# FP4 quantisers of a two-layer audio tower: the rounding constant sized by ScalarE, in a new order of all engines

## The reference, cut to what matters

```python
_GRID = [0.0, 0.5, 1.0, 1.5, 2.0, 3.0, 4.0, 6.0]
_MID  = [0.25, 0.75, 1.25, 1.75, 2.5, 3.5, 5.0]

def fp4_quant_dequant(x):                       # blocks of 16 along the last dim
    scale = max(max(abs(xb)) / 6.0, 1e-12)
    xn = xb / scale
    q = _GRID[searchsorted(_MID, abs(xn))] * sign(xn) * scale

h = silu(fp4_linear(x, w_gate)) * fp4_linear(x, w_up)     # 256 -> 704
return fp4_linear(h, w_down)                              # 704 -> 256
```

## Time and profile before

| | |
|---|---|
| median of 3 runs | 325.51 us (325.51 to 326.44) |
| profiled execution | span 326.4 us, own time 326.44 us |
| TensorE busy | 303.4 us, 5142 matmuls |
| VectorE busy | 240.5 us, 519 instructions |
| ScalarE busy | 121.4 us, 267 instructions |
| GpSimd busy | 26.1 us |
| mean granted TensorE clock | 0.989 |

### The profile page before, as it was taken

One profiled execution on the slowest core, in us unless ns is written; L12 is line 12 of the kernel. 1 busy time (PEld: TensorE's weight loads), 2 busy tenths in 40 slices (PEclk: granted clock), 3 DMA queues, 4 the chain that ended last, 5 costly groups with the idle time before them and its releaser, 6 DMA issues.

```text
span 326.4 us, 11811 instructions
## 1 busy us (share of the span) xinstructions
PE 303.4 (93%) x5142; PEld 265.7 (81%) x5142; DVE 240.5 (74%) x519; ACT 121.4 (37%) x267; POOL 26.1 (8%) x50
## 2 busy tenths in 40 slices
...
GB/s 244 323 329 262 1 3 100 34 4 2 2 52 19 2 4 2 2 1 2 16 21 4 2 4 2 2 4 3 5 16 18 2 4 4 5 0 0 2 0 64
DMA packets 8821, 12.80 MB, mean 39 GB/s; under 512 B 826, under 2 KB 5698, under 8 KB 8772
## 3 DMA queue, kind: packets, MB, share of 16 engines
q1 hardware_dynamic: 8772, 12.06, 11.2%
...
...
## 4 chain that ended last, share of the span: by engine, by line
PE 81%; DVE 10%; DMA 3%; issue 3%; ACT 1%; SPq 1%; POOL 0%; DVEq 0%; ACTq 0%
PE psum L1226 71%; PE psum L1416 2%; DMA ffw_raw<-in_L_ffn_aux_weight_dram 2%; PE psum L1542 2%; PE psum L1438 1%; DMA tokw_raw<-in_L_tok_W_dram 1%; PE psum L1297 1%; PE psum L1322 1%; DVE qs L846 1%; DVE hha L849 1%; DVE qma L1174 1%; PE psum L1253 1%; PE psum L1345 1%; ACT qma L759 1%; PE psum L1519 1%
## 5 line engine op out<-in xcount | busy, mean ns | idle before, releaser
L555 POOL TENSOR_TENSOR ln_rs<-ln_mv,minus_half 128x1 f32<-128x1 f32 x40 | 24.9, 628 | 262.4 <-DVE ln_mv L917 262.4
L1226 PE MATMUL psum<-aT_hi,wqkv_hi 128*128 128x256 f32 x128 | 37.5, 293 | 0.4 <-DVE xT_lo L865 0.2
L1226 PE MATMUL psum<-aT_lo,wqkv_hi 128*128 128x256 f32 x128 | 36.1, 282 | 0.0
L1226 PE MATMUL psum<-aT_hi,wqkv_lo 128*128 128x256 f32 x128 | 35.9, 280 | 0.0
L570 ACT ACTIVATE qkT<-psum 128x512 f32<-128x512 f32 x32 | 18.9, 598 | 36.2 <-PE psum L1226 36.0
L1226 PE MATMUL psum<-wout_s,oT 128*128 128x256 f32 x128 | 29.4, 383 | 0.0
L1226 PEld LDWEIGHTS psum<-wout_s,oT 128*128 128x128 f32 x128 | 23.7, 190 | 3.4
L1226 PEld LDWEIGHTS psum<-aT_hi,wqkv_hi 128*128 128x128 f32 x128 | 24.1, 188 | 1.2 <-issue 0.9
L1226 PEld LDWEIGHTS psum<-aT_lo,wqkv_hi 128*128 128x128 f32 x128 | 24.1, 188 | 0.0
L1226 PEld LDWEIGHTS psum<-aT_hi,wqkv_lo 128*128 128x128 f32 x128 | 24.1, 188 | 0.0
L1226 PE MATMUL psum<-bias_parts,pick_r 128*128 128x256 f32 (+1 forms) x40 | 15.1, 378 | 6.2 <-DVE tokw_lo L865 1.6
...
## 6 DMA issues: line engine op xcount, KB each, us to landing
...
w_raw<-in_L_attn_W_qkv_dram SPq DMA_DIRECT2D x1, 768.0 KB, 10.2
...
```

Source lines behind the costliest of these rows:

```text
L555: nc.gpsimd.tensor_tensor(ln_rs[:, s, k, j:j + 1], ln_mv[:, s, k, j, 1:2], minus_half[:, :], ALU.pow).then_inc(rstd_ready[f"{k}_{j}"], 1)
L1226: return nc.tensor.matmul(o_, a, b, start=first, stop=last)
```

## The change

Steps d and e go. ScalarE computes m = |v| * (2^22 - 1) from the scaled v in one ACTIVATE with Abs, for all four kinds of array: `size_w` (w0e, w1e, w2e in ScalarE's list), `size` (ye and he). VectorE's f becomes max(m, MAGIC) + v and g becomes max(m, MAGIC) - v, the negative of the rounded value, so h multiplies by -1 and by the scale. f, g and h are scalar_tensor_tensor everywhere. VectorE's c signals ScalarE (`scaled`), and f waits for ScalarE (`sized`). A memset on GpSimd and the exponents' semaphores go. All five lists are new: the same steps otherwise, 304 of TensorE, 234 instead of 223 of ScalarE, 388 instead of 418 of VectorE, 41 of GpSimd and 11 of the DMA queue.

```diff
 MAGIC = 1.5 * 2.0 ** 22
+TO_MAGIC = 2.0 ** 22 - 1.0
 BELOW_ONE = float(np.float32(1 - 2.0 ** -24))
...
-        turn_tok xT0.0 bcast warm5 tok0.0 warm3 xT1.0 warm4 tok1.0 warm2 xT0.1 warm1 warm0 turn_ff tok0.1 aT.0
-        join_ff1 xT1.1 qk7.0 qk1.0 tok1.1 qk3.0 v00.0 v01.0 v12.0 qk4.0 qk0.0 qk5.0 v02.0 qk2.0 v11.0 qk6.0
...
+        warm5 warm3 turn_tok xT0.0 xT1.0 warm4 tok0.0 bcast tok1.0 warm2 warm1 xT0.1 warm0 aT.0 turn_ff tok0.1
+        xT1.1 join_ff1 qk1.0 qk7.0 tok1.1 qk3.0 v12.0 v01.0 qk4.0 v00.0 qk5.0 qk0.0 v02.0 qk2.0 v10.0 qk6.0
...
+        g0_1.3 hT0_0.2 g1_1.3 u0_1.3 hT1_0.2 u1_1.3 hT0_1.2 down_0.2 hT1_1.2 hT0_0.3 down_1.2 hT1_0.3 down_0.3
+        hT0_1.3 tail3 hT1_1.3 down_1.3 tail0 tail2""",
...
+        tables turn_tok xT0.0 xT1.0 split_qkv2 bcast split_qkv0 split_qkv3 split_qkv1 split_qkv4 split_b xT0.1
+        aT.0 split_qkv5 turn_ff xT1.1 qk1.0 qk7.0 qk3.0 v12.0 v01.0 qk4.0 v00.0 w0e qk5.0 qk0.0 v02.0 join_ff1
+        qk2.0 v10.0 qk6.0 v11.0 xT0.2 s0.0 e0.0 aT.1 turn_gate1 w1e join_ff2 v00.1 split_w1 s1.0 oT00.0 w2e
+        qk4.1 e1.0 qk3.1 qk6.1 qk2.1 turn_gate0 qk5.1 oT01.0 qk0.1 qk7.1 qk1.1 turn_up1 s0.1 turn_up0 e0.1
...
+        ye_0.2 o1T_0.3 exp1_1.3 o1T_1.2 val1_1.3 yT_0.2 ye_0.3 g0_0.2 g1_0.2 yT_0.3 ye_1.2 o1T_1.3 g0_0.3 yT_1.2
+        g1_0.3 g0_1.2 g1_1.2 ye_1.3 he_0.2 yT_1.3 he_1.2 g0_1.3 g1_1.3 hT0_0.2 he_0.3 hT1_0.2 hT0_1.2 hT1_1.2
+        hT0_0.3 he_1.3 hT1_0.3 hT0_1.3 hT1_1.3""",
...
+        turn_tok xT0.0 split_tokb tokA0.0 xT1.0 split_qkv2 split_qkv0 tokA1.0 tokB0.0 tokC0.0 tokB1.0 tokC1.0
+        st1_0.0 st1_1.0 ln1_0.0 ln1_1.0 xT0.1 split_qkv3 aT.0 tokA0.1 tokB0.1 split_qkv5 xT1.1 split_b
+        split_qkv1 split_qkv4 tokA1.1 tokB1.1 w0a w0b tokC1.1 st1_1.1 w0c tokC0.1 st1_0.1 w1a w1b w0f w0g w0h
+        xT0.2 w1c ln1_0.1 ln1_1.1 s0.0 w2a turn_gate1 aT.1 tokA0.2 mixA0.0 mixB0.0 tokB0.2 mixC0.0 w2b w2c
+        split_w1 s1.0 turn_gate0 w2f mixA1.0 w1f w1g w1h out0.0 st2_0.0 mixB1.0 w2g mixC1.0 turn_up1 s0.1
...
+        sa1_0.3 ya_1.3 sb0_0.3 yb_1.3 sb0_1.2 yc_1.3 sb1_0.3 sa1_1.2 yf_1.3 sb1_1.2 yg_1.3 hf_0.2 ha_1.2 ha_0.3
+        yh_1.3 hg_0.2 hb_1.2 yT_1.3 hc_1.2 hb_0.3 hh_0.2 hf_1.2 sa0_1.3 hg_1.2 hc_0.3 hh_1.2 sa1_1.3 hf_0.3
+        hg_0.3 sb0_1.3 hh_0.3 sb1_1.3 ha_1.3 hb_1.3 hc_1.3 hf_1.3 hg_1.3 hh_1.3 down_1.2 down_0.3 down_0.2
...
-        load.2 wout load.3 store_0.0 store_1.0 store_0.1 store_1.1 store_0.2 store_1.2 store_0.3 store_1.3""",
+        load.2 wout load.3 store_0.0 store_1.0 store_1.1 store_1.2 store_0.1 store_0.2 store_0.3 store_1.3""",
...
-        minus_magic = sb("minus_magic", [P, 1])
...
+        scaled, sized = ({k: sem(f"{n_}_{k}") for k in ("w", "y0", "y1", "h0", "h1")} for n_ in ("scaled", "sized"))
...
-            nc.gpsimd.memset(minus_magic[:, :], -MAGIC).then_inc(filled["minus_magic"], 1)
-            pool.wait_ge(filled["minus_magic"], 1)
...
-            def he(j):
-                def stage(i):
-
-                    act.wait_ge(exponents[j], i + 1)
-                    act.wait_ge(filled["minus_magic"], 1)
-                    nc.scalar.activation(of("qm", i, j)[:, :], of("qm", i, j)[:, :], ACT.Relu, bias=minus_magic[:, :],
-                                         scale=MAGIC).then_inc(magic[j], 1)
+            def size(k, j, buf, cols):
+                def stage(i):
+                    act.wait_ge(scaled[f"{k}{j}"], i + 1)
+                    v = of(buf, i)[:, j, :] if k == "y" else of(buf, i, j)[:, 0:cols]
+                    nc.scalar.activation(of("qm", i, j)[:, 0:cols], v, ACT.Abs,
+                                         scale=TO_MAGIC).then_inc(sized[f"{k}{j}"], 1)
+                return stage
+
+            def size_w(w):
+                def stage(i):
+                    v = FP4[w][1]
+                    act.wait_ge(scaled["w"], w + 1)
+                    nc.scalar.activation(wq_m[:, 0:v.shape[1]], v, ACT.Abs, scale=TO_MAGIC).then_inc(sized["w"], 1)
                 return stage
 
...
-            def fp4(name, arrays, then, by_act=None):
+            def fp4(name, arrays, then, k_, count):
 
 
                 def step(k, needs, op):
@@ -824,42 +826,33 @@
                     st.after("s", name, i)
                     st.done(nc.vector.reciprocal(inv, scale), "b", name, i)
 
-                def exponents_out(i):
+                def scaled_out(i):
                     v, blocks, m_, s_ = arrays(i)
-                    st.after("c", name, i)
-                    nc.vector.tensor_scalar(m_.bitcast(U32), v.bitcast(U32), 0x7F800000, None,
-                                            ALU.bitwise_and).then_inc(exponents[by_act], 1)
+                    st.after("b", name, i)
+                    nc.vector.scalar_tensor_tensor(
+                        out=in_blocks(v), in0=in_blocks(v), scalar=BELOW_ONE, in1=over_blocks(s_[:, 1, 0:blocks]),
+                        op0=ALU.mult, op1=ALU.mult).then_inc(scaled[k_], 1)
 
                 def add_magic(i):
                     v, blocks, m_, s_ = arrays(i)
-                    dve.wait_ge(magic[by_act], i + 1)
-                    st.done(nc.vector.scalar_tensor_tensor(out=v, in0=m_, scalar=MAGIC, in1=v, op0=ALU.add,
+                    dve.wait_ge(sized[k_], count(i))
+                    st.done(nc.vector.scalar_tensor_tensor(out=v, in0=m_, scalar=MAGIC, in1=v, op0=ALU.max,
                                                            op1=ALU.add), "f", name, i)
 
                 def take_magic(i):
                     v, blocks, m_, s_ = arrays(i)
                     st.after("f", name, i)
-                    st.done(nc.vector.scalar_tensor_tensor(out=v, in0=v, scalar=MAGIC, in1=m_, op0=ALU.subtract,
+                    st.done(nc.vector.scalar_tensor_tensor(out=v, in0=m_, scalar=MAGIC, in1=v, op0=ALU.max,
                                                            op1=ALU.subtract), "g", name, i)
 
                 return {
                     "a": step("a", None, lambda v, vb, m_, scale, inv, wide: nc.vector.tensor_reduce(
                         scale, vb, AX.X, ALU.max, apply_absolute_value=True)),
                     "b": scales,
-                    "c": step("c", "b", lambda v, vb, m_, scale, inv, wide: nc.vector.scalar_tensor_tensor(
-                        out=vb, in0=vb, scalar=BELOW_ONE, in1=inv.unsqueeze(2).broadcast_to(wide),
-                        op0=ALU.mult, op1=ALU.mult)),
-                    "d": step("d", "c", lambda v, vb, m_, scale, inv, wide: nc.vector.tensor_scalar(
-                        m_.bitcast(U32), v.bitcast(U32), 0x7F800000, None, ALU.bitwise_and)),
-                    "e": step("e", "d", lambda v, vb, m_, scale, inv, wide: nc.vector.tensor_scalar(
-                        m_, m_, 1.0, MAGIC, ALU.max, ALU.mult)),
-                    "f": step("f", "e", lambda v, vb, m_, scale, inv, wide: nc.vector.tensor_tensor(
-                        v, v, m_, ALU.add)),
-                    "g": step("g", "f", lambda v, vb, m_, scale, inv, wide: nc.vector.tensor_tensor(
-                        v, v, m_, ALU.subtract)),
-                    "h": step("h", "g", lambda v, vb, m_, scale, inv, wide: nc.vector.tensor_tensor(
-                        vb, vb, scale.unsqueeze(2).broadcast_to(wide), ALU.mult)),
-                    **({} if by_act is None else {"d": exponents_out, "f": add_magic, "g": take_magic})}
+                    "c": scaled_out, "f": add_magic, "g": take_magic,
+                    "h": step("h", "g", lambda v, vb, m_, scale, inv, wide: nc.vector.scalar_tensor_tensor(
+                        out=vb, in0=vb, scalar=-1.0, in1=scale.unsqueeze(2).broadcast_to(wide),
+                        op0=ALU.mult, op1=ALU.mult))}
...
-                steps = fp4(f"w{w}", lambda i: (v, v.shape[1] // BLOCK, wq_m[:, 0:v.shape[1]], wq_s[:, w]), w_quantised)
+                steps = fp4(f"w{w}", lambda i: (v, v.shape[1] // BLOCK, wq_m[:, 0:v.shape[1]], wq_s[:, w]), w_quantised,
+                            "w", lambda i: w + 1)
 
                 def first(i):
                     dve.wait_ge(ld[k], 16 if k == "down" else 32)
                     dve.wait_ge(filled["raw_rows"], 1)
                     steps["a"](i)
 
-                def masks(i):
-                    if w:
-                        dve.wait_ge(w_quantised, w)
-                    steps["d"](i)
-                return {f"w{w}{k}": f for k, f in {**steps, "a": first, "d": masks}.items()}
+                return {f"w{w}{k}": f for k, f in {**steps, "a": first}.items()}
...
-                                               qs[:, which(i), j]), y_ready[j])
+                                               qs[:, which(i), j]), y_ready[j], f"y{j}", lambda i: i + 1)
...
-                                               qs[:, which(i), j]), hq_ready[j], by_act=j)
+                                               qs[:, which(i), j]), hq_ready[j], f"h{j}", lambda i: i + 1)
```

(5 more changed lines are left out.)

135 lines of the change are left out of this document (60 added, 75 removed).

## The result

| | before | changed |
|---|---|---|
| median | 325.98 us (325.51 to 326.45, 4 runs) | 333.24 us (331.25 to 335.15, 4 runs) |
| ratio | | 1.0209, 95% interval 1.016 to 1.0257 |
| profiled execution | span 326.4 us, clock 0.989 | span 331.6 us, clock 0.969 |

The account below looks back on a forecast made before the run. Loads bound the start, TensorE the middle, VectorE the tail. Savings of 3.0 (tail) + 0.6 (loads) + 1.6 (middle) = 5.2 us from 326.4 gave 321.2; the forecast was 321.0 us, range 318.2 to 324.8.

Parts of the forecast that it names:

- The middle: TensorE's stage, 30 to 268 us: new lists gain 1.6 us, half of a 3.2 us gap with its low clock.
- My own test: Sign in the next profile: the prediction is wrong if the middle shows low clock more than once.
- The tail: VectorE's last stage, from 268 us: d and e leaving its queue save 3.0 us, between 1.5 and 4.3.
- h's 1.4 us: Part of the tail: d of four h tiles leaves VectorE, 1.3 us for three and 0.1 for the last.
- y's 1.6 us: Part of the tail: d and e of four y tiles leave VectorE's queue, 0.20 us a place, 1.6 us.
- The rule on VectorE: Skill's rule on relu, max, add, mul: by it y's 1.6 us in the tail would bring nothing; the forecast kept them.
- The loads' stage: First 30 us: x's second load issued some 5 us earlier and aT.0 before turn_ff, 0.6 us gained, at most 1.8.
- Smaller saving: Rival: one tile's chain and TensorE's products set the tail, y gives nothing, the middle keeps its gap; 324.4 us, chance 0.19.
- Slower: Rival: ScalarE stands at w1e or w2e, TensorE stops 1.5 us or more, low clock follows; 329.2 us, chance 0.07.
- The tables: Rival: Abs needs another ACT_TABLE_LOAD, two per size on ScalarE, 20 us in the tail; about 341 us, chance 0.02.
- The signs: Wrong if VectorE's tail waits before f exceed 1.5 us, low clock recurs in the middle, or TensorE's products set the end.
- Durations: Abs of about 0.38, 0.8 to 0.88 and 1.4 to 1.48 us; VectorE busy about 226.5 us, ScalarE 128 to 129.

Follow-up runs that it names:

- e1: Changed kernel with the old lists, steps d and e struck and the sizes put into ScalarE's list: 324.54 us, ratio 0.991 against the kernel before.
- e7: e1 with two small mix steps moved on TensorE alone, so that at most three small steps stand together near 170 us: 325.57 us, ratio 0.9983.
- e14: Kernel before with only h's quantiser new (Abs in place of the Relu, d off VectorE's list): 324.74 us, ratio 0.9956.
- e13: Kernel before with only y's quantiser new (d and e off VectorE's list, Abs on ScalarE): 326.09 us, ratio 0.9992.
- e8: Kernel before with six added steps of small matmuls that wait for nothing, in one run on TensorE: 347.94 us, ratio 1.0672.
- e9: Kernel before with the same six added steps as e8, each placed between large steps: 339.38 us, ratio 1.0403.
- e11: Changed kernel with its new lists only up to down_1.0 (163 us), behind it e1's order on every engine: 323.85 us, ratio 0.9924.

## Why the prediction was wrong

- *The middle* is the step that failed: "a gap without a releaser has no cause that I can see removed", and 1.6 us as the most that new lists could lose. The gap did have a cause, and the row was a sample of it: 128 matmuls in less than 3.46 us. e1 has the same gap at the same place, and in e7 it is gone once the small steps around it are spread. Even the gain was priced too high: the low clock behind the gap, 1.7 of the 3.2 us, is missing in e14, e13, e8 and e9, which have the old list there. I read that the lists were new and "TensorE's work is the same", and never looked at how they group small matmuls. From down_1.0 to proj_1.3 before takes 125.8 us (124.0 in e13), the changed kernel 134.0: 8.2 us lost for 1.6 gained. How much of it is stops for instructions with their low clock, and how much the order of the other steps, is open: spreading gave back 3.3 us at most. My own test, low clock more than once in the middle, came out (175, 195 and 267 us).
- *The tail*, 3.0 us, mis-sized: 1.6 us with the old lists by the traces (63.24 - 61.65). h's 1.4 us were right (1.3 measured). y's 1.6 us were not there (0.1). I priced four of VectorE's places, but three of the four y tiles stand before proj_1.3, where TensorE is the bound; only the fourth gave its 0.4 us. Waits at y's f are not the reason: the changed kernel has two of them, 1.37 us before 129.72 and 0.48 before 209.75, both of passes 0 and 1, and none in the tail. That behind hT0_1.2 nothing is won was right: from there to hT0_1.3 it is 10.1 us in before, e1, e13 and e14.
- *The rule on VectorE.* The Trainium skill ("ScalarE: Activation LUTs", section "Rules for kernel authors") puts max and mul on VectorE, not on ScalarE. Following it for y would have left out the 1.6 us, and e13 agrees (ratio 0.9992); in h ScalarE had done a step already, so e14 doesn't test it.
- *The loads' stage*, 0.6 us: x's load came earlier and aT.0 by 2.0 us, but the wait of 2.54 us for ln1 and the low clock behind it (from 21.5 us) left 0.4 at qk1.0. e11 against e1 is 0.7 us, within their intervals. The size was near; that the end gains by it isn't shown, since by the ratios e11 (0.9924) is no better than e1 (0.991).
- *Rival "Smaller saving"* is what the quantisers alone do: 324.4 forecast, 324.54 measured for e1. Its mechanism holds (y gives next to nothing, the gap stays); that the number fits so well is luck, for it counts 0.6 us of the loads' stage, which e1 doesn't have, and starts from the long execution's span. *Rival "Slower"* came nearest in time (329.2) and was wrong in its place: nothing is lost up to 163 us, so w1e and w2e hold nobody up. Its second half, stops of 1.5 us with low clock behind, was right. *The tables* rival falls: one ACT_TABLE_LOAD.
- *The signs.* VectorE's waits before f came to 0.9 us in the tail, under the 1.5 that would have told against me; only the low clock did.
- *Durations* held to within a tenth: Abs 414 ns at 256 columns, 788 at 704, 1492 and 1373 for the weights, where 380, 800 to 880 and 1400 to 1480 were given, ScalarE 128.6 us, VectorE 229.2 (226.5 forecast).
- *The range.* My own lower ends together (tail 1.5, loads 0, middle -1.6) give 326.4 + 0.1 = 326.5 us; the range stopped at 324.8, and the result lies far beyond both. That the sum stood on an execution 2.4 us above the median one made little difference beside the rest.
